# Expert slots of a whole layer in one list of 35 steps in place of two lists of 19

## The chip, the cores and the metric

The kernel runs on one core of a Trainium2 chip. The metric is the time of one execution on the device, in microseconds (us). A core has five engines with a queue of instructions each: TensorE (PE in the profile, its weight loads PEld), VectorE (DVE), ScalarE (ACT), GpSimd (POOL) and SyncE (SP), which here issues nearly all plain DMAs. Engines wait for each other by semaphores and each runs its own instructions in order.

## The reference

The input x has 2 x 2048 tokens of 256 values: 4096 tokens, 32 tiles of 128. Three layers follow one another, all in float32:

```
x = x + 0.5 * ffn(layernorm(x))
x = x + attention(layernorm(x))
x = x + 0.5 * ffn(layernorm(x))        (the same weights as the first)

ffn(h):  g   = softmax(layer_norm(h) @ router_w.T)      4 experts
         top two experts of each token, weights divided by their sum
         hid = relu(layer_norm(h @ w1[e]))              256 -> 512
         out = sum over the two of weight * (hid @ w2[e])  512 -> 256
         return layer_norm(out)
```

Attention is linear and causal, with 16 heads of 16. The change touches the two ffn layers.

## The kernel before

**Slots.** Each token is computed only for its two experts. A token and one of its experts make a slot, so a layer has 8192 slots. The rows of the tokens, split into a high and a low half-precision part, are scattered by indirect DMAs to `slots_in` in DRAM, where every expert has a region of its own. Two blocks of 128 slots of one expert are a slot tile (S2 = 256), and one step of the mixture computes one slot tile. Its results go to `slots_out`; later each token gathers its two rows and sums them with its weights.

**Two groups.** The 32 token tiles of a layer are two groups of 16 (GT). Each group has tables and buffers of its own. 16 token tiles fill 16 slot tiles, and since each expert's last one is only part filled, up to three more are needed: a group has NJ = 19 steps, whatever the router chooses, and a mixture has NP = 38. The list of a group (`tables`: expert and row of each step, read by SP and PE from `rtab` and `etab`) is made once all 16 tiles are routed. Four pads of zeros (`pads`) fill what is left of each expert's last slot tile.

**A step** p, by engine:
- SP stores the two halves of step p-1 (`store_slots`, L480), then loads step p+5 (`load_slots`): two transposed copies to hT (L466) and one plain copy to hs (L469). The first load of a group also writes the pads (L452) and waits for all scatters of the group (L461, L462). R_HT = 5 buffers hold hT, R_HS = 3 hs, R_Y = 4 the results.
- PE runs `grams` of p+2 (L1869, L1870) for the variance of the hidden row, `layer1` of p in two halves (L1893 to L1895), `std_T` of p+1 (L1881), and `layer2` of p-1 in two halves (L1908 to L1910), interleaved.
- DVE runs `variances` of p+2 (L915, L920), `relu_low` (L934), `std_parts` (L926, L927) and `twice_low` of p+3 (L906).
- ACT runs `relu_high` (L1451, two a step), `std_row` (L1444) and `scale_out` of p-1 (L1459).
- POOL raises the variances to a power, `pair_std` (L613).

**Beside the steps.** In the 19 steps of a layer's first group the second group is routed, one or two token tiles a step (`ROUTED`, steps 0 to 9): statistics for four tiles at a time (`quad_norm` L782 and L785, `quad_factors`), rows on ACT (L1420, L1427), their low part on DVE (L801), four transposes on PE with a copy by ACT (`row_T`, L1433), and logits. After an octet of tiles (steps 5 and 10) come `logits`, `choose`, `place`, then `scatter` of two tiles a step on POOL (two indirect DMAs a tile, L605), in steps 7 to 10 and 12 to 15. `tables` follows at step 12, `positions` and `gates` at step 13. In the steps of the second group the first group's outputs leave, one tile a step: `gather` (L629) on POOL, `first_weighted` (L1468) on ACT, `token_sum` and `token_out` on DVE (L950 to L965).

The first group of the first layer is routed in the preparation, together with the preparing of the weights (`weights`). The first group of the second layer is routed within attention, where the second group of the first layer leaves as well; its rows lie where W2 was, so that W2 is fetched again from DRAM afterwards (L501). The last group leaves in a tail after the last step (`gather_last`). In the first mixture `ahead` prepares attention: maxima and scales of its weights at steps 14 to 18, rows of its first tokens in the second group's steps (`rs` on POOL, L1606 on ACT, `rows_out_T` on PE, L1977).

Of SP's order before the change, the core is:

```
for p in range(p0, p1):
    if p > p0:
        store_slots(p - 1, 0)
        store_slots(p - 1, 1)
    if p + AHEAD < p1:
        load_slots(p + AHEAD)
```

## Time and profile before

| what | value |
|---|---|
| median of 3 runs | 1131.0 us (1130.91 to 1135.23) |
| profiled execution | 1138.73 us |
| its span | 1137.0 us |
| mean granted TensorE clock | 0.901 of full |
| busy: PE, DVE, ACT, POOL | 872.4, 732.4, 500.6, 561.3 us |
| bytes read from DRAM and written | 50.89 MB, 47.19 MB |

The span runs from the first to the last instruction of the program in the profiled execution; the time has what lies around it as well, and this execution was among the longer ones. "Busy" is time in which an engine has an instruction at work; waits of the sequencers and issuing of DMAs aren't counted. Matmuls overlap each other, so the mean duration of one, about 275 ns, is not its share of the time.

### The profile page before, as it was taken

The numbers are of one execution on the slowest core, as the hardware profiler recorded it, in microseconds if no ns is written. First come the engines' busy times: TensorE is split into PE (matmuls) and PEld (weight loads), VectorE is DVE, ScalarE is ACT, GpSimd is POOL, SyncE is SP. The second block draws the span as 40 slices with busy tenths as digits, with TensorE's granted clock in tenths as the row PEclk, the third lists the DMA queues.
The fourth block names the chain that finished last, engine by engine and source line by source line (L and its number), as shares of the span: only waits on it lengthen the run. The fifth ranks groups of instructions, "written<-read, shape, count | busy, mean of one in ns | idle before, by whom it ended". The sixth has DMA issues, their size and how long they took to land.

```text
span 1137.0 us, 26666 instructions
## 1 busy us (share of the span) xinstructions
PE 872.4 (77%) x8596; PEld 662.4 (58%) x8596; DVE 732.4 (64%) x2104; ACT 500.6 (44%) x958; POOL 561.3 (49%) x631
## 2 busy tenths in 40 slices
PE   1543499978999897798788787775799989999700
PEld 1432387856888774565555554443687778888500
DVE  4547776666777754598787764372675774878335
ACT  2642366422444454565565555430565333444311
POOL 4146224551456453687685366354226542555373
PEclk9956599999999998999899899995899999999955
DMA  8042654563566411111121112123645657666343
GB/s 296 10 158 111 157 155 127 152 168 106 130 158 163 130 63 24 40 40 46 43 51 46 23 44 68 31 77 107 159 103 158 155 154 155 163 159 151 118 131 107
DMA packets 191146, 126.06 MB, mean 111 GB/s; under 512 B 126373, under 2 KB 180905, under 8 KB 190633
## 3 DMA queue, kind: packets, MB, share of 16 engines
q1 hardware_dynamic: 177746, 89.72, 30.1%
q0 software_dynamic: 12288, 33.57, 10.1%
q8 instruction: 79, 1.29, 0.5%
q10 hardware_dynamic: 984, 1.07, 0.3%
q14 instruction: 49, 0.40, 0.1%
HBM read 50.89 MB, written 47.19 MB: 86 GB/s over the span
## 4 chain that ended last, share of the span: by engine, by line
PE 48%; DVE 14%; issue 13%; POOL 7%; ACT 6%; DMA 5%; SPq 3%; another core or an unknown queue 3%; ACTq 0%; DVEq 0%; POOLq 0%
PE banks L1908 4%; PE banks L1895 4%; PE banks L1893 4%; PE banks L1894 4%; PE banks L1910 4%; PE banks L1909 4%; PE banks L1993 4%; POOL slots_in L605 3%; PE banks L1995 3%; PE banks L2106 3%; PE banks L1994 3%; PE banks L1869 2%; PE banks L1870 2%; DMA area<-slots_out,pos 2%
## 5 line engine op out<-in xcount | busy, mean ns | idle before, releaser
L613 POOL TENSOR_TENSOR stds<-vare,expo 128x4 f32<-128x4 f32 x76 | 80.5, 1059 | 208.3 <-DVE vare L920 207.0
L1908 PE MATMUL banks<-w2all,area 128*128 x608 | 167.0, 275 | 6.3 <-DMA w2all<-w_kept 3.6
L1893 PE MATMUL banks<-area,w1h 128*128 128x256 f16 x608 | 169.1, 278 | 2.1 <-DVE area L934 1.9
L1895 PE MATMUL banks<-area,w1l 128*128 128x256 f16 x608 | 168.5, 277 | 0.9 <-issue 0.9
L1894 PE MATMUL banks<-area,w1h 128*128 128x256 f16 x608 | 168.9, 278 | 0.3 <-issue 0.2
L1910 PE MATMUL banks<-w2all,area 128*128 x608 | 166.7, 274 | 1.8 <-issue 1.8
L1909 PE MATMUL banks<-w2all,area 128*128 x608 | 166.7, 274 | 0.0
L934 DVE SCALAR_TENSOR_TENSOR area<-banks,area 128x512 f16<-128x512 f32 x152 | 104.4, 687 | 88.2 <-ACT area L1451 75.2
L1451 ACT ACTIVATE area<-banks 128x512 f16<-128x512 f32 x152 | 89.6, 590 | 123.8 <-PE banks L1895 99.8
L605 POOL DMA_INDIRECT slots_in<-area,spos x96 | 102.9, 1072 | 75.4 <-DVE spos L855 49.6
L737 POOL TENSOR_TENSOR area<-area 128x512 f16<-128x512 f32 x64 | 79.3, 1244 | 119.0 <-ACT area L1663 118.4
L1459 ACT ACTIVATE area<-banks,stds 128x256 f32<-128x256 f32 x152 | 70.9, 466 | 98.6 <-PE banks L1910 80.3
L629 POOL DMA_INDIRECT area<-slots_out,pos x96 | 97.0, 1010 | 25.8 <-issue 21.6
L1993 PE MATMUL banks<-area 64*128 64x32 f16 (+1 forms) x766 | 76.6, 226 | 41.5 <-issue 21.5
L1869 PE MATMUL banks<-gramh,area 128*128 x304 | 77.9, 290 | 24.9 <-issue 11.0
L1993 PEld LDWEIGHTS banks<-area 64*128 64x128 f16 (+1 forms) x766 | 39.9, 96 | 77.7 <-issue 51.0
L915 DVE CUSTOM_DVE_ANT_0 area<-banks,area 128x256 f16<-128x256 f32 x152 | 58.3, 420 | 33.0 <-PE banks L1870 27.2
L1995 PE MATMUL banks<-area 64*128 64x32 f16 (+1 forms) x766 | 75.9, 221 | 4.5 <-issue 4.5
L1870 PE MATMUL banks<-graml,area 128*128 x304 | 77.9, 291 | 0.6 <-issue 0.6
L1994 PE MATMUL banks<-area 64*128 64x32 f16 (+1 forms) x766 | 75.5, 222 | 2.2 <-issue 2.2
L1663 ACT ACTIVATE area<-area 128x512 f16<-128x512 f32 x64 | 40.1, 628 | 71.1 <-DVE area L1325 68.4
L1908 PEld LDWEIGHTS banks<-w2all,area 128*128 128x128 f16 x608 | 59.5, 98 | 19.5 <-issue 7.5
(278 smaller groups left out, 2226.3 us busy)
## 6 DMA issues: line engine op xcount, KB each, us to landing
area<-slots_in SPq DMA_DIRECT2D x76, 256.0 KB
slots_out<-area SPq DMA_DIRECT2D x152, 128.0 KB
X<-in_L_attn_x_dram SPq DMA_DIRECT2D x8, 512.0 KB, 6.1
slots_in<-zrow SPq DMA_DIRECT2D x16, 256.0 KB
area<-area SPq DMA_DIRECT2D x256, 16.0 KB
out_dram<-X SPq DMA_DIRECT2D x32, 128.0 KB
area<-slots_in SPq DMA_TRANSPOSE x152
area<-in_L_ffn_w_dram SPq DMA_DIRECT2D x4, 512.0 KB, 11.7
```

Of the source, the lines that this page charges most:

```text
L605: pool.indirect_dma_start(slots_in[G % 2], bass.IndirectOffsetOnAxis(spos[:, O % 2, k, j:j + 1], 0), rows_of(i).rearrange("p c d -> p (c d ...
L934: dve.scalar_tensor_tensor(out=Rl[:, p % 2, ms].rearrange("p m t -> p (m t)"), in0=bank[k][:, :], scalar=0.0, in1=Rh[:, p % 2, ms].rearran ...
L1869: pe.matmul(o, a[:, c], gramh[c][:, bass.ds(e, 1), :], start=(c == 0), stop=False)
L1893: pe.matmul(o, w1h[c][m][:, bass.ds(e, 1), :], a[:, c], start=(c == 0), stop=False)
L1894: pe.matmul(o, w1h[c][m][:, bass.ds(e, 1), :], a[:, KC + c], start=False, stop=False)
L1895: last = pe.matmul(o, w1l[c][m][:, bass.ds(e, 1), :], a[:, c], start=False, stop=(c == KC - 1))
L1908: pe.matmul(o, Rh[:, p % 2, k, rows], w2h[k][:, bass.ds(e, 1), :], start=(k == 0), stop=False)
L1909: pe.matmul(o, Rh[:, p % 2, k, rows], w2l[k][:, bass.ds(e, 1), :], start=False, stop=False)
L1910: last = pe.matmul(o, Rl[:, p % 2, k, rows], w2h[k][:, bass.ds(e, 1), :], start=False, stop=(k == HC - 1))
L1993: pe.matmul(o, lh, rh, start=start, stop=False, **kw)
L1994: pe.matmul(o, lh, rl, start=False, stop=False, **kw)
L1995: return pe.matmul(o, ll, rh, start=False, stop=stop, **kw)
```

## The change

A layer has one list of NP = NT + E - 1 = 35 steps for all its 32 token tiles, one `slots_in` and one `slots_out`. The list is made in three pieces, each as soon as its slots are certain:
- after the first octet, 8 token tiles: steps 0 to 4, slot tiles that this octet fills;
- after the second, 16 token tiles: steps 5 to 12, those filled by then;
- after all four: steps 13 to 34. It begins with the slot tiles that were part filled by the first 16 token tiles, so that by step 18 all slots of these are done, and the first half's outputs can leave from step 20.

The load of a step waits for the piece of the list and the scatters that it needs. The pads come once a layer, at SP's step 9, and slot tiles 13 and 14 are loaded at its step 10, each later one four steps ahead. Routing of the second half is done in steps 0 to 5, three token tiles a step (in order 3, 3, 2, 3, 3, 2), with the first rows ahead of step 0; octets are complete at steps 2 and 5, scatters take three tiles a step in steps 4 to 9, and the last tables are made at step 8. Two banks take turns for the transposed rows. On PE, `std_T` now stands ahead of `layer1`. The first half leaves in steps 20 to 32, two tiles in three of them. In attention the first octet gets its tables ahead of the second. The reload of W2 follows the first five loads as before, but waits for the scatters of attention by itself. `ahead` keeps its step numbers (the former second group's count on from 19, less three), and a spare region of zeros is written once at the start, for slot tiles past the last.

```diff
-    NJ = GT + E - 1
-    NP = 2 * NJ
-    REG = GT * P + S2
+    NO = NT // TO
+    NP = NT + E - 1
+    SPARE = NT * P + S2
+    REG = SPARE + (E - 1) * S2
+    PHASE = (0, TO - E + 1, GT - E + 1, NP)
+    SEGS = (1, 3, 4)
+    K1 = GT + E - 1
...
-        ROUTED = (0, 2, 3, 5, 6, 8, 10, 11, 13, 14, 16)
-        OCTET_AT = (5, 10)
-        C_AT = 1
+        ROUTED = (0, 3, 6, 8, 11, 14, 16)
+        OCTET_AT = (2, 5)
+        MOVED = (3, 3, 2)
+        LEFT = (2, 1, 1, 2, 1, 1, 2, 1, 1, 1, 1, 1, 1)
+        LAST_AT = 10
...
+        def started(j):
+            return ROUTED[max(0, min(j + 2, len(ROUTED) - 1))]
         def routed(j):
+            return range(started(j - 1), started(j))
+        def leaves(j):
+            k = j - K1 - 1
+            return range(sum(LEFT[:k]), sum(LEFT[:k + 1])) if 0 <= k < len(LEFT) else ()
...
             def load_slots(p):
+                f, j = p // NP, p % NP
+                if j in PHASE:
+                    sp.wait_ge(r_tab, 3 * f + PHASE.index(j) + 1)
+                if j == PHASE[0]:
+                    sp.wait_ge(sc_h[0], 32 * TO * (2 * f + 1))
+                if j == PHASE[1]:
+                    sp.wait_ge(sc_h[1], 32 * TO * (2 * f + 1))
+                if j == PHASE[2]:
                     for o in range(GO):
+                        sp.wait_ge(sc_h[o], 32 * TO * (2 * f + 2))
+                    sp.wait_ge(sc_p, 16 * E * (f + 1) + 16)
...
+            def load_at(j):
+                return j - AHEAD if j < PHASE[2] else max(j - AHEAD, LAST_AT, j - 4)
...
                 else:
+                    for o in range(GO):
+                        sp.wait_ge(sc_h[o], 32 * TO * 3)
                     sp.wait_ge(m_w2, 16)
                     sp.dma_start(w2flat, w2_kept).then_inc(m_w2, 16)
+                for j in range(NP):
+                    if j > 0:
+                        store_slots(p0 + j - 1)
+                    if j == LAST_AT - 1:
+                        pads(f)
+                    for i in range(NP):
+                        if load_at(i) == j:
+                            load_slots(p0 + i)
...
 (POOL, mixture)
+                for j in range(NP):
+                    if j < GQ:
+                        quad_again(Q1 + j)
+                    if j + 2 < NP:
+                        pair_std(p + 2)
+                    if j + 2 < GQ:
+                        quad_rstd(Q1 + j + 2)
+                    for t in moves(j):
+                        scatter(GT * (G + 1) + t)
+                    for t in leaves(j):
+                        gather(GT * G + t)
+                    for t in leaves(j - 1):
+                        token_rstd(GT * G + t)
...
 (DVE, mixture; the loop over j, in its order)
                 quad_norm(Q1)
+                quad_norm(Q1 + 1)
                 twice_low(p0)
...
+                    for t in leaves(j - 2):
+                        token_out(i0 + t)
+                    if j + 2 < NP:
+                        variances(p + 2)
+                    for t in tiles[:1]:
+                        row_low(i0 + GT + t)
                     relu_low(p, 0)
+                    if j == 0 and f == 0:
+                        positions(G)
+                    if j == 1 and f == 0:
+                        gates(G)
+                    if j == OCTET_AT[-1] + 3:
+                        tables(f, 2)
+                    if j == OCTET_AT[-1] + 4:
+                        positions(G + 1)
...
 (DVE, the preparation)
                 chain(0)
+                tables(0, 0)
...
                 chain(1)
-                tables(0)
+                tables(0, 1)
...
 (ACT, mixture)
+                    for t in leaves(j - 1):
+                        first_weighted(i0 + t)
+                    if j + 1 < NP:
+                        std_row(p + 1)
                     relu_high(p, 0)
...
 (PE, mixture)
+                    if j + 2 < NP:
                         e[p + 2] = expert(p + 2)
                         grams(p + 2, e[p + 2])
+                    if j + 1 < NP:
+                        std_T(p + 1, i1 + started(j - 2))
                     layer1(p, 0, e[p])
+                    for t in turn[:1]:
+                        pe.wait_ge(b_sdr, p + 2)
+                        row_T(i1 + t)
+                    if j > 0:
                         layer2(p - 1, 0, e[p - 1])
+                    for t in turn[1:2]:
+                        row_T(i1 + t)
+                    layer1(p, 1, e[p])
+                    for t in turn[2:]:
+                        row_T(i1 + t)
```

The new `tables` and `positions` work on the limits of these pieces (4, 12 or 16 numbers) and on all steps at once; `positions` has six operations on 192 or 256 elements, the last `tables` three on 352.

## Rows read from the trace of the kernel before

**Rows 1.** The page: the span, and TensorE's busy time.
```profile
span 1137.0 us, 26666 instructions
...
PE 872.4 (77%) x8596; PEld 662.4 (58%) x8596; DVE 732.4 (64%) x2104; ACT 500.6 (44%) x958; POOL 561.3 (49%) x631
```

**Rows 2.** Stages: length, busy PE, PEld, DVE, ACT, POOL, PE's clock, DMA share, GB/s.
```profile
0.00:134.00 134.00, 50.07 (x319) 38.85 (x320) 80.58 (x251) 49.63 (x89) 52.04 (x81) 0.76 0.43 141
...
829.00:901.00 72.00, 68.51 (x698) 57.15 (x697) 46.31 (x184) 39.01 (x80) 32.77 (x32) 1.00 0.55 138
946.00:1070.00 124.00, 122.60 (x1124) 104.56 (x1123) 87.26 (x270) 52.58 (x110) 59.55 (x65) 1.00 0.59 144
1070.00:1137.00 67.00, 1.85 (x17) 1.42 (x15) 27.60 (x84) 7.76 (x18) 35.26 (x36) 0.55 0.43 131
```

**Rows 3.** Timeline of PE: start, duration, instruction; first grams of two steps.
```profile
323.04 0.27 PE L1869 MATMUL banks<-gramh,area 128*128 x1
...
329.57 0.27 PE L1869 MATMUL banks<-gramh,area 128*128 x1
```

**Rows 4.** Groups of ACT, 829 to 901: count, busy, mean ns, idle before.
```profile
L1451 ACT ACTIVATE area<-banks 128x512 f16<-128x512 f32 x19 | 11.3, 595 | 21.0 <-PE banks L1895 13.8 <-remote 6.5 <-issue 0.7
...
L1433 ACT ACTIVATE area<-banks 128x512 f16<-128x512 f16 x11 | 6.5, 589 | 0.0
L1420 ACT ACTIVATE h<-X,xnr,xrs 128x256 f32<-128x256 f32 x10 | 5.9, 592 | 0.0
```

**Rows 5.** Windows, L1451 (relu_high) alone: length, busy (count), clock, DMA.
```profile
901.00:947.00 46.00, 7.16 (x12) 0.96 0.55 153
```

**Rows 6.** Waits from 797 to 829: total, times, longest.
```profile
PE banks L1908 <- DMA w2all<-w_kept: 3.6, 1, 3.6
```

**Rows 7.** Timeline of SP's queue at the second mixture's start.
```profile
782.00 2.60 SPq L466 DMA_TRANSPOSE area<-slots_in  x2
...
800.85 0.46 SPq L501 DMA_DIRECT2D w2all<-w_kept  x1
```

**Rows 8.** Chain that ended last, at the end of the preparation: start, length.
```profile
125.36 1.42 DVE xst L782 x4
126.80 0.39 DVE xmv L785 x4
```

**Rows 9.** Windows, the stretch of the first tables on DVE.
```profile
86.40:90.60 4.20, 0.00 (x0) 0.00 (x0) 3.68 (x23) 0.34 (x1) 2.87 (x3) 0.90 0.45 155
```

**Rows 10.** Groups of POOL, 853 to 930.
```profile
L605 POOL DMA_INDIRECT slots_in<-area,spos x32 | 34.4, 1074 | 13.7 <-issue 8.3 <-DVE spos L855 5.4
L613 POOL TENSOR_TENSOR stds<-vare,expo 128x4 f32<-128x4 f32 x10 | 10.7, 1073 | 16.5 <-DVE vare L920 16.4
```

**Rows 11.** Timeline of SP, two steps of the first mixture's second half.
```profile
319.31 2.53 SPq L466 DMA_TRANSPOSE area<-slots_in  x2
...
325.39 2.54 SPq L466 DMA_TRANSPOSE area<-slots_in  x2
```

**Rows 12.** Timeline of SP, pads and first load of the last list.
```profile
920.07 4.67 SPq L452 DMA_DIRECT2D slots_in<-zrow  x4
927.78 2.72 SPq L466 DMA_TRANSPOSE area<-slots_in  x2
```

**Rows 13.** Chain that ended last: landing of that load's second transpose.
```profile
929.31 2.68 DMA area<-slots_in
```

**Rows 14.** Windows around a stop of PE, columns as in rows 2.
```profile
249.00:254.00 5.00, 0.56 (x4) 0.09 (x2) 4.77 (x7) 0.47 (x1) 3.96 (x4) 0.96 0.82 241
254.00:257.00 3.00, 2.59 (x13) 1.86 (x14) 0.53 (x3) 0.00 (x0) 0.00 (x0) 0.50 0.73 251
```

**Rows 15.** Chain that ended last: gathers that it waited for.
```profile
364.07 4.56 DMA area<-slots_out,pos
...
959.14 5.59 DMA area<-slots_out,pos
```

**Rows 16.** Timeline of DVE: the twice_low that waited for that load.
```profile
933.80 0.69 DVE L906 SCALAR_TENSOR_TENSOR area<-area 128x512 f32<-128x512 f16 x1 [2.38 <-DMA area<-slots_in]
```

More of the change, by code:

```diff
@@ L1188, in mixture @@
                     relu_low(p, 1)
-                    if here and octet(j, 1) is not None:
+                    if octet(j, 1) is not None:
                         place(O1 + octet(j, 1))
+                    for t in tiles[2:]:
+                        row_low(i0 + GT + t)
+                    if octet(j, 0) is not None:
+                        logits(O1 + octet(j, 0))
                     if f == 0:
-                        ahead(g - G, j)
-                    if p + 3 < p0 + NP:
+                        ahead(j)
+                    if j + 3 < NP:
                         twice_low(p + 3)
@@ L1786, in router @@
                 if j == 0:
-                    wait(pe, r_cnt, O - 1)
+                    wait(pe, r_cnt, O - 1 if O < GO or beside(i) else O)
                 if i == 0:
```

444 lines of the change are left out of this document (210 added, 234 removed).

## The prediction

> **What bounds the kernel now.** First the page's header and TensorE's line [rows 1]: TensorE works 77% of a span of 1137.0 us. Such a mean hides the stages, so the table by stage is next [rows 2]: preparation to 134, the first mixture's 38 steps, attention, the second mixture to about 1070, and a tail of 67 us in which TensorE does next to nothing. In 946 to 1070 TensorE is busy 122.6 of 124 us at full clock: it bounds a step that has no routing in it. Its length is read from the first gram matmul of two steps [rows 3]: 329.57 - 323.04 = 6.53 us. From 829 to 901 there are 19 relu_high (two a step), so 9.5 steps in 72 us, 7.6 each [rows 2, 4]; ten tiles are routed there, so a tile costs (72 - 9.5 x 6.53) / 10 = 1.0 us with all its stalls. The steps in which the second half's list begins are longer: 901 to 947 has 12 relu_high, six steps, in 46 us, 6.8 above 6 x 6.53 [rows 5]. Preparation, attention and the tail are chains through several engines.
>
> **The change, part by part.** The sum is made against the profiled execution, 1138.7 us, which is 7.7 above the median of the runs shown (1131.0); the difference is then taken from the median.
>
> *Steps.* A mixture runs 35 instead of 38, in both layers: 6 x 6.53 = **-39.2** [rows 3]. The loads, stores, pair_std and ReLU work of these steps go with them, all beside TensorE.
>
> *W2 of the second layer.* TensorE waits 3.6 us for the reload [rows 6]. SP issues it at 800.85, behind the ten transposes that it began at 782.00, when the last scatter of attention had landed [rows 7]. The first five loads need only the first octet after the change, so SP has them out before that wait, and the reload follows it at once: **-3.6**. TensorE is not free of attention before 786, so nothing more is gained there.
>
> *The old boundary.* Its 6.8 us in the second mixture [rows 5] held pads, scatter wait and slow scatter steps; they are priced anew below, so **-6.8** (between 0 and -6.8). In the first mixture the same steps carry the attention scales, which stay at steps 14 to 17: 0.
>
> *Preparation.* quad_norm of a second quad now stands on VectorE before the first twice_low: statistics 1.42 and aggregation 0.39, 1.9 us with the guard, on the chain [rows 8]. There is a table more (for one octet), some 18 short VectorE instructions, as many as the old table, in whose stretch VectorE was busy 3.68 of 4.2 us [rows 9]. It stands where VectorE also waits for others, so I take half: 1.9. Together **+4** (1.9 to 7).
>
> *Routing three tiles a step.* In all the 16 tiles cost TensorE the same. ACT makes two row activations (L1420, and L1427 of the same size) and a copy (L1433) per tile, 0.59 each [rows 4]. Three tiles add 5.3 us to at most 52.58 / 19 = 2.8 us of a plain step [rows 2]: 8.1 us, just under TensorE's 6.53 plus its part of three tiles. In the first mixture VectorE also has positions in step 0, with six larger operations more. **+4** for both layers (0 to 12).
>
> *Scatters.* Three tiles are six indirect DMAs. 32 of them took 34.4 us with 8.3 us between them, 1.33 each; a pair_std takes 1.07 [rows 10]. That is 9.1 us of POOL a step, against 6.5 of TensorE in steps 7 and 8. pair_std stands first in POOL's step and is needed only in the next one, some 4 us later, which covers most of it: **+1** (0 to 10). Here a rule speaks against the change. In the rows the scatters run beside a VectorE that is busy 46.31 of 72 us, and their mean is 1.07 [rows 2, 10]: little blocking is seen. The Trainium skill, SBUF — State Buffer, section "SBUF: two separate sides", says that VectorE and GpSimd share one port pair under an exclusive lock, and that GpSimd can't write the descriptors of its DMAs while VectorE holds it. By the row the term is +1; by the rule it grows to that of rival D.
>
> *Tile 13.* The largest loss. SP writes the pads at step 9, behind the stores of tile 8, and loads tiles 13 and 14 only at step 10. SP gets to its load 2.35 us after the next TensorE step begins (325.39 against 323.04), or 2.8 (319.31, where the step began at 323.04 - 6.53 = 316.51) [rows 3, 11]. From the first pad to the load behind the pads it is 927.78 - 920.07 = 7.7 us [rows 12]. So the load of 13 begins 2.8 + 7.7 = 10.5 us after step 10 does, 4.0 into step 11; without pads it would be 2.8. It has landed at 929.31 + 2.68 = 931.99, 4.2 after its issue [rows 12, 13]. The grams of tile 13 are TensorE's first work of step 11, so it stops for 7.0 to 8.2 us, 7.5 taken. Behind them stand std_T, both layers, and so ACT, VectorE and the stores; nothing covers it. When TensorE had been busy 0.56 of 5 us (249 to 254), the granted clock stood at 0.50, the 1.2 GHz level, from 254 to 257 [rows 14]; 2.6 us of work at half speed lose 1.3. Two layers: 2 x 8.8 = **+17.5** (0, if work of other engines had stopped TensorE anyway, to 22).
>
> *Loads four ahead.* From tile 13 on, tile i is loaded at step i-4, not i-5. From the start of a TensorE step the load begins at 2.35 to 2.8 and lands 4.2 later, at 6.55 to 7.0; it is needed at 6.53 [rows 3, 11, 13]. A whole step of spare is gone; these two would be 0.0 and 0.5 late, 0.25 in the mean. Of 2 x 22 such steps, eight of the first mixture stand beside other stalls: 36 x 0.25 = **+9** (0 to 25).
>
> *Gathers.* 16 tiles leave in 13 steps, so some steps gather two. Two landings of a gather are on the chain now, 4.56 and 5.59 us [rows 15]. A second tile puts two more issues, 2 x 1.3 if they cost what a scatter does [rows 10], before the landing that ACT waits for: at step 21 of both mixtures and behind rs(0) of the first, at most 7.8, taken **+6** (0 to 14).
>
> *Attention.* Two tables for one on VectorE, the second longer: **+1** (0 to 4).
>
> Sum: -39.2 - 3.6 - 6.8 + 4 + 4 + 1 + 17.5 + 9 + 6 + 1 = -7.1. Profiled execution 1131.6; median 1131.0 - 7.1 = 1124.
>
> **The rivals.** (A) *Most of the gain stays.* If tile 13 and the loads four ahead cost nothing, since routing makes steps 7 to 10 slow enough for SP and POOL to keep up, the sum is -33.6: 1098. Against it: SP's order is fixed, and the store before the load needs layer 2 of the step before. Chance 0.16.
> (B) *Slower.* Place: the slot rows (hs), copied behind the two transposes. VectorE began twice_low at 933.80 on rows whose load began at 927.78, 6.0 us [rows 12, 16]. With four ahead they come 8.4 to 8.8 us after the start of a step, 1.9 to 2.3 into the step whose variances need them, and VectorE, in order, stands still before relu_low, token sums and std_parts. It decides when that outruns TensorE's slack. VectorE is busy 87.26 of 124 us in the second mixture's second half [rows 2], and its 16 tiles will fall on fewer steps. If each of the 44 steps loses 0.7, none hidden, it is 30.8 - 9 = 21.8 more: 1146; at 0.5, 1137. Chance 0.27.
> (C) *No difference to see.* The same terms, each stall somewhat larger (10 us at tile 13, 0.35 a step): 1131. Chance 0.19.
> (D) *The lock.* If a scatter is blocked about as long again as it takes, 32 x 1.0 us more a mixture, all on the way to tile 13, less what TensorE's spare covers, it is about +50: 1174. It is the mechanism of the skill page named above. Chance 0.04.
> That the change doesn't do what it says is no case: the counts of steps are constants in it.
>
> **How the numbers follow.** The forecast's own case (1109 to 1125) has 0.34. A measurement of this kernel can tell about 0.5%, 5.7 us, from no change. Faster: 0.34 + 0.16 = 0.50; same 0.19; slower 0.27 + 0.04 = 0.31. The range for 8 in 10 goes from 1098 (A) to 1146 (B at its full price).
>
> **What would show it.** 70 pair_std instead of 76; no wait for W2; at step 11 of each mixture grams that wait 7 to 8 us for slots_in, behind the zrow stores; steps of 6.5 to 7 from 13 on, with waits for slots_in; waits for gathers at steps 21 and 27. The forecast is wrong if the wait at step 11 is under 3 us, if the later steps take over 7.1, or if preparation grows by over 8.

## The result and the profile after

The kernel after takes 1169.6 us (median of 4 runs, 1166.0 to 1178.3); the kernel before, on the same chip, 1133.1 (4 runs). The ratio is 1.032, interval 1.025 to 1.040: slower by 36.5 us, where 7 us faster was forecast. The profiled execution took 1167.67, that of the kernel before 1138.73, so these two differ by 28.9 us where the medians differ by 36.5. Below, every ratio is taken against the kernel before on the same chip, and its difference from 1 times 1131 us is "its us".

The page of the kernel after, where the first two lines answer to [rows 1]:

```profile
span 1165.9 us, 25520 instructions
...
PE 852.1 (73%) x8236; PEld 636.6 (55%) x8236; DVE 734.1 (63%) x2108; ACT 491.8 (42%) x928; POOL 550.6 (47%) x625
```

TensorE stands still for 49 us more (span less busy time). Its busy time falls by 20 us only, though it runs 360 matmuls less, 60 a step, which at full clock are 39 us of work (122.60 us for 1124 matmuls in [rows 2]). By stage, from the first relu_high of a mixture to the first one of its last step (us):

```
            preparation  first mixture  attention  second mixture  tail   span
before         136.6         279.4        382.8        266.2       72.0  1137.0
after          138.7         299.5        382.7        272.4       72.6  1165.9
```

Of the 28.9 us of span, 26.3 are in the two mixtures, which have three steps less and are 20.1 and 6.2 us longer. The windows of the two mixtures, columns as in [rows 2], first of the kernel before, then of the kernel after:

```profile
136.60:416.00 279.40, 257.82 (x2385) 213.97 (x2383) 195.43 (x626) 128.24 (x262) 129.53 (x147) 0.97 0.54 139
798.80:1065.00 266.20, 251.70 (x2361) 210.75 (x2360) 182.38 (x597) 120.83 (x248) 120.47 (x122) 0.99 0.58 147
```

```profile
138.70:438.20 299.50, 251.59 (x2202) 203.41 (x2201) 190.69 (x607) 120.67 (x240) 123.22 (x143) 0.91 0.47 123
821.00:1093.00 272.00, 239.06 (x2172) 195.56 (x2170) 171.81 (x550) 112.81 (x225) 112.61 (x118) 0.96 0.48 129
```

The granted clock falls from 0.97 and 0.99 to 0.91 and 0.96. Since its levels are 1.0 and 0.5, the time at 0.5 (1.2 GHz) is twice what the mean lacks to 1, times the length: an estimate of 22 us before and 76 after. So a stop costs twice here, once as waiting and again when TensorE works on at 1.2 GHz behind it. About half of the 39 us that the removed steps saved went back in this way. But for tile 13 no term below shows it separately; in the experiments it is part of each time.

Step lengths, each from the first gram matmul of a step to that of the next, as in [rows 3], show where the steps grew:

```
first mixture, steps 0 to 10
before   9.1  7.1  7.7  7.1  7.7  7.9  7.5  7.9  7.5  8.7  6.8
after    9.5  9.7  7.3 10.0 14.0  9.2 10.1  6.6 10.0 14.8 13.5
steps 20 to 31
before   6.5  6.5  6.5  6.5  6.5  6.5  6.5  6.5  6.5  6.5 11.3  8.0
after    6.7  6.9 11.3  8.2  6.5  8.2  7.4 15.5  7.3  6.5  6.7  6.5

second mixture, steps 0 to 10
before   9.0 12.5  7.8  7.1  7.7  7.9  7.4  7.7  7.7  9.4  6.8
after    9.2  8.1  7.3 10.0  9.8  9.0 11.8  6.6  9.9 13.7 13.3
steps 20 to 31, where outputs leave
before   6.5  6.5  8.0  6.5  6.5  6.5  6.5  6.5  6.5  6.5  6.5  6.5
after    6.5  7.5  8.4  6.5  8.4 11.5  7.8  6.6  7.8  7.1  6.8  7.1
```

The plain steps between (13, 17 to 20 of the second mixture) are 6.5 to 6.6 again. Its step 1 has lost W2's wait of [rows 6] and is 4.4 us shorter.

**Tile 13.** The waits of the kernel after from 905 to 930 (total, times, longest), then SP's queue in the same stretch, which answers to [rows 12]:

```profile
PE banks L1942 <- DMA area<-slots_in: 6.4, 1, 6.4
```

```profile
914.38 3.59 SPq L471 DMA_DIRECT2D slots_in<-zrow  x4
918.01 1.51 SPq L503 DMA_DIRECT2D slots_out<-area  x2
920.75 2.55 SPq L489 DMA_TRANSPOSE area<-slots_in  x2
```

The grams of step 11 wait behind pads, stores and load, in that order: 6.4 us here and 6.8 in the first mixture, for 7 to 8.2 foreseen. Step 11, behind the wait, runs in part at 1.2 GHz and takes 8.8 and 8.6 us for a plain 6.5, with a granted clock of 0.72 in both; here the second:

```profile
924.80:933.40 8.60, 8.38 (x58) 6.43 (x59) 2.84 (x10) 2.26 (x4) 1.01 (x1) 0.72 0.39 105
```

**What was not foreseen** stands in front of it. GpSimd's queue in the kernel after, at its steps 7 and 8 of the second mixture: twelve scatters (L635) in two runs of six about one pair_std:

```profile
887.89 1.04 POOL L635 DMA_INDIRECT slots_in<-area,spos  x1 [0.20 <-issue]
...
894.30 0.96 POOL L635 DMA_INDIRECT slots_in<-area,spos  x1 [0.30 <-issue]
895.28 1.04 POOL L642 TENSOR_TENSOR stds<-vare,expo 128x4 f32<-128x4 f32 x1
896.52 1.04 POOL L635 DMA_INDIRECT slots_in<-area,spos  x1 [0.20 <-issue]
...
902.93 0.96 POOL L635 DMA_INDIRECT slots_in<-area,spos  x1 [0.30 <-issue]
```

TensorE in the same stretch, and ACT's relu_high:

```profile
893.20 0.27 PE L1968 MATMUL banks<-area,w1l 128*128 128x256 f16 x1
893.59 0.27 PE L1981 MATMUL banks<-w2all,area 128*128 x1
894.98 0.27 PE L1982 MATMUL banks<-w2all,area 128*128 x1 [1.12 <-issue]
895.09 0.27 PE L1983 MATMUL banks<-w2all,area 128*128 x1
895.71 0.27 PE L1981 MATMUL banks<-w2all,area 128*128 x1 [0.35 <-issue]
896.43 0.28 PE L1982 MATMUL banks<-w2all,area 128*128 x1 [0.45 <-issue]
...
903.18 0.58 PE L1954 MATMUL banks<-ident,s 128*1 128x128 f16 x4 [3.33 <-DVE s L988]
```

```profile
896.47 0.60 ACT L1522 ACTIVATE area<-banks 128x512 f16<-128x512 f32 x1 [5.19 <-remote]
...
905.19 0.60 ACT L1522 ACTIVATE area<-banks 128x512 f16<-128x512 f32 x1 [5.30 <-remote]
```

The window of that stretch, columns as in [rows 2]:

```profile
893.00:896.00 3.00, 1.39 (x9) 0.56 (x6) 0.00 (x0) 0.00 (x0) 2.64 (x3) 1.00 0.70 226
```

Until 893.2 a matmul follows the other every 0.11 us. Then, at full clock and with no wait named, matmuls start singly or in twos, 0.7 or 1.4 us apart, and relu_high comes 5.6 us after the matmul that it reads (L1968 at 890.58). This is called slow issue below. The second thing is the last line of TensorE's rows: std_T, which now stands ahead of layer1, waits 3.3 us for VectorE. VectorE's queue tells why:

```profile
897.10 0.69 DVE L995 SCALAR_TENSOR_TENSOR area<-banks,area 128x512 f16<-128x512 f32 x1 [6.73 <-issue]
897.71 0.15 DVE L888 TENSOR_TENSOR cnt<-carry,regbase 128x4 f32<-128x4 f32 x1
...
902.73 0.17 DVE L987 TENSOR_SCALAR s<-stds 128x2 f16<-128x2 f32 x1
902.93 0.20 DVE L988 SCALAR_TENSOR_TENSOR s<-stds,s 128x2 f16<-128x2 f32 x1
```

The last `tables`, 5.1 us, stands ahead of std_parts (L987, L988), which std_T needs. It begins so late because relu_low (L995) stands before it, which begins as the late relu_high ends.

The kernel before has the slow issue as well, where it scatters two tiles a step. TensorE and ACT in its first mixture, at the end of step 13 and in step 14:

```profile
238.52 0.27 PE L1870 MATMUL banks<-graml,area 128*128 x1 [0.38 <-issue]
239.25 0.27 PE L1869 MATMUL banks<-gramh,area 128*128 x1 [0.47 <-issue]
```

```profile
240.75 0.47 ACT L1459 ACTIVATE area<-banks,stds 128x256 f32<-128x256 f32 x1 [6.27 <-remote]
```

ACT stood idle for 6.27 us. So what the change adds is more of it, not something new.

**Gathers.** Waits of the kernel after from 1000 to 1093, then from 330 to 425. ACT waited for landings before as well (43.8 us in 16 times from 946 to 1066). New is that TensorE then waits for std_parts (L988), 6.9 us in each mixture, and in the first, at step 27, 6.1 us for the rows for attention (3.5 before).

```profile
ACT area L1539 <- DMA area<-slots_out,pos: 34.6, 13, 4.2
...
PE banks L1954 <- DVE s L988: 6.9, 5, 3.3
```

```profile
ACT area L1539 <- DMA area<-slots_out,pos: 31.9, 13, 6.5
...
PE banks L2048 <- ACT h L1680: 6.1, 1, 6.1
```

### The profile page after: what moved, and what is told of

The parts are those of the page before. It is cut to its first block, busy times and chain, and to the rows that moved or that the text cites. A ratio compares the mean times of both kernels' runs of the same rounds, so it can differ in the third digit from the quotient of the medians.

```text
span 1165.9 us, 25520 instructions
## 1 busy us (share of the span) xinstructions
PE 852.1 (73%) x8236; PEld 636.6 (55%) x8236; DVE 734.1 (63%) x2108; ACT 491.8 (42%) x928; POOL 550.6 (47%) x625
## 4 chain that ended last, share of the span: by engine, by line
issue 26%; PE 24%; DVE 17%; POOL 14%; DMA 7%; ACT 6%; SPq 4%; another core or an unknown queue 1%; DVEq 0%; ACTq 0%; POOLq 0%
POOL slots_in L635 5%; POOL stds L642 4%; DMA area<-slots_out,pos 4%; PE banks L2064 3%; PE banks L2177 3%; PE banks L2066 2%; PE banks L2065 2%; DMA area<-slots_in 2%; POOL area L659 2%; SPq L548 2%; PE banks L1824 1%; ACT area L1709 1%; SPq L489 1%; POOL area L718 1%
## 5 line engine op out<-in xcount | busy, mean ns | idle before, releaser
L642 POOL TENSOR_TENSOR stds<-vare,expo 128x4 f32<-128x4 f32 x70 | 73.2, 1045 | 272.0 <-DVE vare L981 272.0
L995 DVE SCALAR_TENSOR_TENSOR area<-banks,area 128x512 f16<-128x512 f32 x140 | 96.3, 688 | 112.0 <-ACT area L1522 82.6
L1967 PE MATMUL banks<-area,w1h 128*128 128x256 f16 x560 | 159.4, 285 | 1.9 <-issue 1.8
L1966 PE MATMUL banks<-area,w1h 128*128 128x256 f16 x560 | 160.1, 286 | 0.5 <-DVE area L995 0.5
L1968 PE MATMUL banks<-area,w1l 128*128 128x256 f16 x560 | 158.9, 284 | 1.4 <-issue 1.4
L1981 PE MATMUL banks<-w2all,area 128*128 x560 | 154.8, 276 | 3.3 <-issue 2.5
L1982 PE MATMUL banks<-w2all,area 128*128 x560 | 154.8, 276 | 2.0 <-issue 2.0
L1983 PE MATMUL banks<-w2all,area 128*128 x560 | 154.6, 276 | 0.6 <-issue 0.4
L635 POOL DMA_INDIRECT slots_in<-area,spos x96 | 97.7, 1017 | 67.2 <-DVE spos L879 39.4
L1522 ACT ACTIVATE area<-banks 128x512 f16<-128x512 f32 x140 | 82.6, 590 | 102.7 <-PE banks L1968 74.0
L1530 ACT ACTIVATE area<-banks,stds 128x256 f32<-128x256 f32 x140 | 65.6, 469 | 88.0 <-PE banks L1983 71.3
L1515 ACT ACTIVATE area<-banks 1x512 f16<-1x512 f16 x70 | 40.6, 580 | 97.6 <-PE banks L1954 79.6
L976 DVE CUSTOM_DVE_ANT_0 area<-banks,area 128x256 f16<-128x256 f32 x140 | 53.7, 421 | 26.9 <-PE banks L1943 14.4
## 6 DMA issues: line engine op xcount, KB each, us to landing
area<-in_L_ffn_w_dram SPq DMA_DIRECT2D x4, 512.0 KB, 11.4
area<-in_L_ffn_w_dram SPq DMA_DIRECT2D x2, 1024.0 KB, 14.8
```

The lines of the kernel that those rows point to most:

```text
L635: pool.indirect_dma_start(slots_in, bass.IndirectOffsetOnAxis(spos[:, O % 2, k, j:j + 1], 0), rows_of(i).rearrange("p c d -> p (c d)"), No ...
L642: pool.tensor_tensor(stds[:, p % R_SD], vare[:, p % 2].unsqueeze(2).to_broadcast([P, 2, 2]), expo[:, :].unsqueeze(1).to_broadcast([P, 2, 2 ...
L1966: pe.matmul(o, w1h[c][m][:, bass.ds(e, 1), :], a[:, c], start=(c == 0), stop=False)
L1967: pe.matmul(o, w1h[c][m][:, bass.ds(e, 1), :], a[:, KC + c], start=False, stop=False)
L1968: last = pe.matmul(o, w1l[c][m][:, bass.ds(e, 1), :], a[:, c], start=False, stop=(c == KC - 1))
L1981: pe.matmul(o, Rh[:, p % 2, k, rows], w2h[k][:, bass.ds(e, 1), :], start=(k == 0), stop=False)
```

## Experiments: the parts on the kernel before

Each of these puts one part of the change on the kernel before.

**Scatters of three tiles a step.**

```diff
 def moves(j):
-    if at + 2 <= j < at + 2 + TO // 2:
-        t = TO * o + 2 * (j - at - 2)
-        return t, t + 1
+    k = j - at - 2
+    if 0 <= k < 3:
+        return tuple(range(TO * o + 3 * k, TO * o + min(3 * k + 3, TO)))
```

> The kernel before, with its scatters three token tiles a step (3, 3, 2 in steps 7 to 9 and 12 to 14) and nothing else changed. Theory S (six indirect DMAs of POOL in a row, twelve and more in two steps, slow down the issue of instructions on TensorE, ScalarE and VectorE): each of the four octets loses some 3 to 5 us, the kernel is 10 to 20 us slower, with idle time marked issue or remote on PE and ACT while POOL scatters. Rival (the bursts are harmless; in the changed kernel tables and rows hold up the steps): within 3 us, or a few us faster, since the last scatter lands a step earlier.

Measured: 1157.39 us, ratio 1.0216 (1.0173 to 1.0258): +24.4. Steps 8 and 14 take 16.0 and 19.5 us in the first mixture, 15.5 and 18.5 in the second, for 7.5, 16.5, 7.7 and 11.1. GpSimd's own work, six scatters at 1.27 and a pair_std, is 8.7 us a step and can't make 16. TensorE of this kernel in step 14 of the second mixture, in the middle of its grams:

```profile
924.33 0.27 PE L1870 MATMUL banks<-graml,area 128*128 x1 [0.39 <-issue]
925.05 0.27 PE L1869 MATMUL banks<-gramh,area 128*128 x1 [0.45 <-issue]
926.47 0.27 PE L1870 MATMUL banks<-graml,area 128*128 x1 [1.15 <-issue]
927.21 0.27 PE L1869 MATMUL banks<-gramh,area 128*128 x1 [0.47 <-issue]
```

The same beat as in the kernel after. It lasts until 935.8, 1.4 us behind the end of the series of scatters. From 928 on the granted clock is 0.50, so the +24.4 hold slow work behind the gaps too.

**Three tiles routed a step**, octets and scatters where they were.

```diff
-ROUTED = (0, 2, 3, 5, 6, 8, 10, 11, 13, 14, 16)
+ROUTED = (0, 3, 6, 8, 8, 8, 11, 14, 16)
```

(and quad_norm, quad_factors and their powers in each step instead of every other one)

> The kernel before with three token tiles routed a step (3, 3, 2, none, none, 3, 3, 2) and the statistics of a quad in each step, the octets, tables and scatters where they were. My prediction priced the dense routing of the kernel after at +4 us for both layers; its first seven steps stood 24 us over the plain steps, with routing itself. Density theory: the six full steps take 10 us or more each, the free ones 6.5, and the sum is 5 to 15 us more, 1136 to 1146. Rival: ACT keeps up, 1131 to 1134.

Measured: 1148.3 us, ratio 1.0100 (1.0074 to 1.0126): +11.3. The steps that route three, three and two tiles take 10.7, 13.4, 8.0 and 10.0, 11.2, 8.9 in the second mixture; step 1 holds the wait for W2, and steps 0 and 1 took 9.0 and 12.5 without this. The time is within the 5 to 15 us expected, while the steps with two tiles stay under the 10 us. The cause shows in the waits: TensorE's transposes (L1777) wait 6.4 and 6.1 us for ACT's copy (L1433) in the two mixtures, for 1.3 and 1.0 in the kernel before.

**Outputs that leave in 13 steps.** `gather`, `first_weighted`, `token_sum` and `token_out` over the tiles of `leaves`, as in the kernel after:

```diff
+LEFT = (2, 1, 1, 2, 1, 1, 2, 1, 1, 1, 1, 1, 1)
...
-    t = j - C_AT
-    if 0 <= t < GT:
-        gather(GT * G + t)
+    for t in leaves(j):
+        gather(GT * G + t)
```

> The kernel before with the outputs leaving in 13 steps, two token tiles in three of them, as in the kernel after. If the density of the gathers made the gather steps of the kernel after slow (they took 21 and 14 us over 6.53 a step, 6 and 1 before), this one loses 10 to 28 us: 1141 to 1159. If the slower gather steps come from the other order of the engines' work or from the four-step loads, it stays at 1131 to 1134.

Measured: 1156.31 us, ratio 1.0166 (1.0133 to 1.0198): +18.8. TensorE's waits in its first mixture, 306 to 425:

```profile
PE banks L1896 <- DVE area L939: 6.0, 2, 4.9
PE banks L1980 <- ACT h L1609: 4.5, 1, 4.5
```

layer1 waits for relu_low (L939), which waits for relu_high, which stands behind the landing; and the rows for attention come late, as at step 27 of the kernel after. The steps one or two behind a pair of tiles take 9.3 and 14.2 us in the first mixture and 8.4, 11.0 and 8.7 in the second, and step 30 of the first 13.8 for 11.3.

**The weighting moved out of the way.** The last kernel, with ACT's `first_weighted` behind both relu_high and scale_out, and `token_sum` behind relu_low.

```diff
 (ACT)
-    for t in leaves(j - 1): first_weighted(i0 + t)
     relu_high(p, 0)
...
     scale_out(p - 1, 1)
+    for t in leaves(j - 1): first_weighted(i0 + t)
```

> The kernel before with the dense gathers (which cost 20 us), where ACT weights the gathered rows at the end of its step instead of ahead of relu_high, and VectorE sums them behind relu_low. If the loss comes from ACT waiting for the landing ahead of relu_high, so that TensorE stands still behind it, most of it goes: 1131 to 1141. If it comes from the gathers themselves (transfers, issue of GpSimd ahead of pair_std), it stays at 1150 to 1156.

Measured: 1152.47 us, ratio 1.0113 (1.0080 to 1.0147): +12.8 for +18.8. The two intervals overlap a little. In the first mixture step 28 falls from 14.2 to 9.3 us and step 30 from 13.8 to 10.4; in the second step 25 falls from 11.0 to 8.0 and step 21 rises from 8.4 to 10.4. So the landing ahead of relu_high is perhaps a third of the price. The rest stays with two tiles of gathers on GpSimd ahead of the next pair_std; which part of them isn't told apart.

**std_T and std_row first.** Before: `std_T` ahead of `layer1`, `std_row` ahead of `relu_high`.

```diff
+    std_T(p + 1, ...)
     layer1(p, 0, e[p])
-    std_T(p + 1, ...)
```

> The kernel before with std_T ahead of layer1 on PE and std_row ahead of relu_high on ACT, as the change has them. Theory T: slower by 8 to 20 us, in the steps of the second half, with waits of PE for the parts of the standard deviation after late gathers. Rival G: within 4 us of the kernel before, since one gather a step is early enough.

Measured: 1141.56 us, ratio 1.0083 (1.0051 to 1.0115): +9.4. That isn't all waiting at std_T: in the profile TensorE waits for std_parts (L927) 1.6 us in the first mixture and 2.3 in the second. The step that grew most, step 9 of the second mixture, 14.2 for 9.4, begins with gram matmuls 0.6 and 0.7 us apart with no wait named, and ACT's relu_high (L1451) starts late there twice, after 1.75 and 2.46 us idle marked remote. What the order costs apart from that isn't shown.

## Experiments: the parts undone in the kernel after

**std_T and std_row back behind.**

```diff
-    std_T(p + 1, i1 + started(j - 2))
     layer1(p, 0, e[p])
+    std_T(p + 1, i1 + started(j - 2))
...
-    std_row(p + 1)
     relu_high(p, 0)
+    std_row(p + 1)
```

> The changed kernel with std_T back behind the first half of layer1 on PE, and std_row back behind relu_high on ACT. Theory T (std_T ahead of layer1 takes from TensorE the 1.3 us in which std_parts used to arrive, so each late gather now stops it): the steps of the second half lose their waits of PE L1954 for DVE L988, 8 to 12 us less in each mixture, about 1150 in all against 1168. Rival G (the gathers two a step are what costs, wherever std_T stands): within 4 us of the changed kernel.

Measured: 1166.74 us, ratio 1.0344 (1.0272 to 1.0417): nothing gained, and the 8 to 12 us a mixture of theory T not there. In the kernel after the order by itself costs nothing that can be told.

**Pads and tile 13 one step earlier.**

```diff
-    if j == LAST_AT - 1:
+    if j == LAST_AT - 2:
         pads(f)
...
-    return j - AHEAD if j < PHASE[2] else max(j - AHEAD, LAST_AT, j - 4)
+    return j - AHEAD if j < PHASE[2] else max(j - AHEAD, LAST_AT - 1, j - 4)
```

> The changed kernel with the pads written at SP's step 8 and slot tile 13 loaded at its step 9. The wait of the grams of tile 13, 6.4 and 6.8 us in the changed kernel, is SP's order: it should shrink by 3 to 6 us in each mixture, 6 to 12 us in all, about 1158. If the wait is set by the scatters' landing instead, it stays above 5 us and the time within 3 us of the changed kernel.

Measured: 1159.21 us, ratio 1.0236 (1.0192 to 1.0280): +26.7, so 9.8 of the 36.5 go. Step 10 falls from 13.5 and 13.3 to 8.5 and 7.7, and step 11 to 6.5 in both. Step 9 of the first mixture grows from 14.8 to 17.1. The intervals of the two kernels overlap a little; the step lengths don't leave the gain in doubt.

**With that, outputs thinned,** the last tile weighted, summed and put out behind the last step:

```diff
-LEFT = (2, 1, 1, 2, 1, 1, 2, 1, 1, 1, 1, 1, 1)
+LEFT = (2,) + 14 * (1,)
```

> The kernel after with the pads and tile 13 one step earlier (1159 by itself) and the first half leaving one tile a step up to the last step, the last tile behind it. If the 20 us that dense gathers cost in the kernel before are the same 20 us here, it comes to about 1140, less what the last tile adds behind the last step (2 to 5 us): 1140 to 1146. If the gather steps of the kernel after are long for another reason, it stays at 1155 or above.

Measured: 1159.99 us beside 1138.73 of the kernel before, ratio 1.0143 (1.0080 to 1.0206): +16.2, 10.5 less than without. That is about half of what dense gathers cost on the kernel before, with intervals that overlap a little; 1140 to 1146 us was expected, so the dense gathers cost less here than there.

**With the pads at step 8, the last octet two tiles a step** in steps 7 to 10, tile 13 at step 10 as in the kernel after:

```diff
-MOVED = (3, 3, 2)
+MOVED = ((3, 3, 2), (2, 2, 2, 2))
```

> The kernel after with the pads at step 8 and tile 13's load left at step 10, and the last octet scattered two tiles a step in steps 7 to 10 instead of three in steps 7 to 9. If six scatters a step make the 14 us steps, those at 9 and 10 fall to under 9 us in both mixtures, and against the kernel with only the pads earlier (1.024 of before) it gains 8 to 14 us less what tile 13 waits for its later scatters (2 to 8 us): 1.012 to 1.022. If they stay at 14 us, the spacing isn't the cause in the kernel after: 1.024 or above.

Measured: 1166.25 us, ratio 1.0302 (1.0237 to 1.0366), +34.2: no gain that can be told against the kernel after, and 7.5 us more than with the pads and tile 13 a step earlier. By what was set down before, this speaks against the spacing of the scatters as the cause in the kernel after. Its steps say more. Step 8 falls to 6.8 and 6.6, for 10.0 and 9.9, and TensorE has no gap without a named wait there, though relu_high still comes 2.8 us behind its matmul (888.80, L1968 at 885.73). But step 9 stays at 13.2 and 13.9 and step 10 takes 15.9 and 15.1. Its waits from 886 to 924:

```profile
PE banks L1942 <- DMA area<-slots_in: 8.4, 1, 8.4
...
PE banks L1954 <- DVE s L988: 4.5, 1, 4.5
```

The first has grown from 6.4, since tile 13's load waits for the last two tiles' scatters, which come a step later. The second is `tables` ahead of std_parts. So on the way to tile 13 the kernel after has three stops behind one another, and thinning one of them uncovers the others. That reading fits the steps; what the six scatters a step cost in the kernel after by themselves is not shown.

## Experiments: what the slow issue needs

All put work beside the kernel before, in the second mixture alone; the scatters write to tensors that nobody reads.

**Six scatters more in each of steps 16 and 17**, in which nothing is routed:

```diff
+if f == 1 and g == G and j in (16, 17):
+    for t in range(3):
+        for k in range(2):
+            pool.indirect_dma_start(more[6 * (j - 16) + 2 * t + k], ..., rows_of(3 * GT + TO + t), None)
```

> The kernel before with twelve more scatters of the usual size (128 rows of 1 KB, to tensors that nobody reads), six in each of steps 16 and 17 of the second mixture, where nothing is routed. Theory S (scatters issued one behind the other by GpSimd slow the issue of all engines): each of these two steps or the one behind grows as in the kernel before with three tiles a step, together 10 to 25 us over the 13 us that two plain steps take; 1141 to 1156. Rival P (GpSimd is merely busy, and pair_std late behind 7.6 us of scatters): 7.6 + 1.1 = 8.7 us a step for 6.5, together 4 to 5 us; 1135. Rival 0: nothing, 1131.

**Six powers of 128x4 on GpSimd instead:**

```diff
+    for t in range(6):
+        pool.tensor_tensor(busy_out[:, 6 * (j - 16) + t], capn[:, 0:4], nhalf[:, :], ALU.pow)
```

> The same steps with six powers of 128x4 numbers a step on GpSimd in place of the six scatters, about 1.06 us each, so 6.4 us of GpSimd and no DMA. Theory S expects no slow issue here: at most 7.5 us a step, 1131 to 1134. Rival P, for which the time of GpSimd is the cause, expects the same loss as with the scatters.

**Scatters of rows of 64 bytes instead** (the source is `rows_of(3 * GT + TO + t)[:, 0, 0:D // 8]`):

> The same twelve scatters with rows of 64 bytes in place of 1 KB: as many descriptors, a sixteenth of the bytes. If the issuing or the descriptors slow the engines (S1), the loss is that of the full scatters, 10 to 25 us. If it is the bytes that fill the DMA engines (S2), the steps stay under 9 us each and the time is 1131 to 1136.

**Twelve plain copies by SP instead,** behind its loads of these steps:

```diff
+    for t in range(6):
+        sp.dma_start(more[6 * (p - p0 - 16) + t], zrow[:, :]).then_inc(s_more, 16)
```

> Twelve plain copies of 128 rows of 1 KB from SBUF to DRAM issued by SP in the same two steps: the bytes of the twelve scatters, none of GpSimd's issuing. S1 expects no slow issue, though SP's own loads may come late: up to 5 us, 1131 to 1136. S2 expects 10 to 25 us as with the scatters.

Measured: 1.0029 (0.9999 to 1.0060), 1.0002 (0.9973 to 1.0031), 1.0021 (0.9979 to 1.0063) and 1.0041 (1.0007 to 1.0075). I expected slow issue from the first; it gave 3 us, near rival P's size, with an interval that holds 0, and none of the four shows single steps over 10.5 there. Step 16 takes 10.2 in the first, but also 10.3 and 10.5 in other kernels of this document that add nothing at that step. Small rows and large ones can't be told apart at this size. By these four my theory would have fallen. Its series holds the same numbers, with one difference:

```profile
921.05 1.04 POOL L669 DMA_INDIRECT more<-area,spos  x1 [0.20 <-issue]
922.39 1.96 POOL L669 DMA_INDIRECT more<-area,spos  x1 [0.30 <-issue]
924.66 0.96 POOL L669 DMA_INDIRECT more<-area,spos  x1 [0.30 <-issue]
```

In each of its two runs of six one scatter took 1.96 us; in the series beside which TensorE went slow all took 0.96 to 1.04. Which is cause and which effect isn't shown, and series with neither stand in the traces too (eight scatters from 883 to 894 in the kernel with the last octet two tiles a step). The window from 930 of the kernel with the twelve large scatters, columns as in [rows 2], shows that a full DMA alone doesn't do it; in the slow stretch of the kernel after the DMA share was 0.70:

```profile
930.00:935.00 5.00, 4.67 (x43) 3.85 (x41) 3.21 (x5) 1.80 (x4) 4.19 (x4) 1.00 0.86 246
```

**Two scatters more beside the four in steps 7 to 9 and 12 to 14**, and the same with two powers in their place:

```diff
+if f == 1 and g == G and j in (7, 8, 9, 12, 13, 14):
+    for k in range(2):
+        pool.indirect_dma_start(more[2 * n + k], ...)
```

> The kernel before with two more scatters of full size (to tensors that nobody reads) in each of steps 7, 8, 9, 12, 13 and 14 of the second mixture alone, behind the four that are there: six a step for GpSimd, as in the kernel before with three tiles a step, but in the steps that route. Theory B (six indirect DMAs a step beside routing slow the issue of all engines, wherever they write): steps 8 and 14 of the second mixture take 14 us or more for 7.5 and 11, the time grows by 10 to 20 us, 1141 to 1151. Rival C (twelve more in plain steps cost 2 to 5 us, so it isn't the number, but something of the real scatters): up to 5 us, 1131 to 1136.

> The same steps with two powers on GpSimd, 1.06 us each, in place of the two scatters. Theory B expects no slow issue and less than 4 us, 1131 to 1135. If it is the lateness of pair_std behind a full GpSimd, the loss is nearly that of the scatters.

Measured: 1161.61 us, ratio 1.0188 (1.0136 to 1.0241), +21.3; and 1140.78 us, 1.0021 (0.9985 to 1.0056). Twelve DMAs that nobody waits for until the end cost about 21 us (15 to 27 by the interval), in steps 8, 10 and 14 (16.7, 11.4 and 16.8 for 7.7, 6.8 and 11.1). Two powers there, about the same time of GpSimd without DMAs, cost nothing that can be told. TensorE of the first of these kernels in step 8:

```profile
868.50 0.27 PE L1918 MATMUL banks<-w2all,area 128*128 x1 [1.17 <-issue]
869.22 0.27 PE L1919 MATMUL banks<-w2all,area 128*128 x1 [0.46 <-issue]
869.93 0.28 PE L1920 MATMUL banks<-w2all,area 128*128 x1 [0.44 <-issue]
```

**Six more in each of steps 3 and 4**, where tiles are routed and nothing else is scattered, and **in steps 24 and 25**, beside gathers. The edit is that of steps 16 and 17 with these conditions (and rows of zeros as the source in the first):

```diff
+if f == 1 and g == G and j in (3, 4):
...
+if f == 1 and g == G + 1 and j in (5, 6):
```

> The kernel before with six more scatters of 1 KB rows (zeros, to tensors that nobody reads) in each of steps 3 and 4 of the second mixture, where three tiles are routed and GpSimd issues no other scatter. If it is routing beside six scatters that slows the issue, two steps there grow by 8 us or more together, as at steps 8 and 14. If it is the length of an unbroken series (steps 12 to 15 and their neighbours hold 16 or more), each grows by under 2.5 us, as in steps 16 and 17.

> Six more scatters in each of steps 24 and 25 of the second mixture, where a tile leaves a step (two gathers and a power more for GpSimd): eight indirect DMAs a step, about 12.4 us of GpSimd for a step of 6.53, and nothing routed. By GpSimd's time alone the two steps and the one behind grow by about 12 us together. If the slow issue needs only the number of indirect DMAs, by 20 us or more, with single steps of 14 us and TensorE's matmuls some 0.7 us apart.

Measured: 1.0062 (1.0037 to 1.0087), +7.0, with steps 4 and 5 at 13.1 and 10.0 for 7.7 and 7.9 and matmuls 0.7 and 1.4 us apart from 826.1 to 829.7. And 1.0100 (1.0043 to 1.0157), +11.3, with steps 25 to 27 at 11.4, 13.4 and 7.9, 13.1 over plain ones. The two steps of the first grow by 7.5 us together, just under the 8 that stood for this theory, and far over the 2.5 each of the other. It says that a series of six beside routing is enough. The second, with two executions only, gives what GpSimd's time alone would; the beat shows in it as well (3.6 us of gaps, 984.6 to 989.8), but the time doesn't need it.

What the runs show: beside six indirect DMAs of GpSimd a step, issued one behind the other, TensorE's issue can be slow for 4 to 12 us; it takes neither the real destination nor readers, and powers in their place don't do it. Open stays why steps 16 and 17 escaped, and by what path it comes about. Plain copies of the same bytes were put only in steps 16 and 17, where the scatters were harmless too, so whether it is GpSimd's issuing or the transfers beside those of a routing step isn't separated.

## Experiment: a version faster than both

The kernel before with two transfers moved: W2's reload behind three of the five first loads, and the second list's pads at SP's step 12.

```diff
 for p in range(p0, p0 + AHEAD):
     load_slots(p)
+    if f == 1 and p == p0 + 2:
+        sp.wait_ge(m_w2, 16)
+        sp.dma_start(w2flat, w2_kept).then_inc(m_w2, 16)
...
-    else:
-        sp.wait_ge(m_w2, 16)
-        sp.dma_start(w2flat, w2_kept).then_inc(m_w2, 16)
...
+    if p == p0 + OCTET_AT[-1] + 2:
+        pads(2 * f + 1)
```

> The kernel before with its two late transfers moved: the pads of the second list at SP's step 12 instead of ahead of its first load at step 14, and the reload of W2 behind three of the five first loads. By the rows of before, 3.6 us of waiting for W2 go, and the first load of the second list comes up to 4.7 us earlier where it is on the path (surely the second mixture, perhaps not the first, where the attention scales are made at the same steps): 1123 to 1128. Rival: that load waits for the last scatter of step 15 and not for the pads, and only the W2 wait goes: 1128. Rival: the reload delays two loads of the first steps by as much: 1131.

Measured: 1127.67 us against 1136.18 of the kernel before on the same chip, ratio 0.9925 (0.9899 to 0.9952): 8.5 us faster. SP's queue at the start of its second mixture:

```profile
793.19 0.46 SPq L490 DMA_DIRECT2D w2all<-w_kept  x1
```

The reload is issued 7.7 us earlier than in [rows 7], and step 1 of the second mixture takes 7.1 for 12.5 us. That is 5.4 of the 8.5; the rest isn't placed, and the interval reaches from 5.4 to 11.4. The pads moved and gained nothing: steps 14 to 17 take 32.7 us for 32.1, for the load waits for the last scatter.

## Why the prediction was wrong

By its own steps:
- *Steps*, -39.2: right; the plain steps are 6.53 us and three fewer a layer. This is TensorE's work at full clock.
- *W2*, -3.6: right and too small. Step 1 is 4.4 us shorter in the kernel after, 5.4 in the version above.
- *The old boundary*, -6.8: not tested by itself. Its steps are gone, but the steps that took its work over are longer than it was.
- *Preparation*, +4: 2.1. *Attention*, +1: 382.7 for 382.8.
- *Routing three a step*, +4 (0 to 12): 11.3 on the kernel before, at the end of its range. I summed ACT's time against TensorE's and took the difference; that TensorE's transposes wait for ACT's copy was not in that sum, and they wait 12.5 us there for 2.3.
- *Scatters*, +1 (0 to 10): 24.4 on the kernel before. **This step failed most.** The working was right about GpSimd, 8.7 to 9.1 us a step. That the other engines go slow beside it was in no term of mine, though the kernel before shows it (ACT idle for 6.27 us at 240.75). In the kernel after the 24.4 aren't shown: there four scatters a step instead of six in one octet gave nothing that can be told.
- *Tile 13*, +17.5 (0 to 22): the waits are 6.8 and 6.4 us where 7.5 was taken. Step 11 behind them is 2.3 and 2.1 over the plain 6.5 at a clock of 0.72, where 1.3 was taken. That makes 17.6, and earlier pads give 9.8 of it back. The mechanism was right.
- *Loads four ahead*, +9: TensorE waits for slots_in in all 9.1 us (3 times) in the first mixture and 11.1 (8 times) in the second, so 7.0 beside tile 13's 13.2. About right. The sign that the later steps take over 7.1 came all the same: steps 13 to 31 of the second mixture are 7.3 us in the mean, by the steps where outputs leave.
- *Gathers*, +6 (0 to 14): 18.8 on the kernel before, 10.5 given back by thinning in the kernel after. I priced the landing alone; layer1 behind relu_low behind relu_high stood 4.9 us in one place.
- Missing altogether: the clock behind every stop but tile 13's. By the estimate above, 22 us of the mixtures ran at 1.2 GHz before and 76 after, tile 13's among them. And std_T ahead of layer1 with the last `tables` ahead of std_parts: the order alone goes with +9.4 on the kernel before and nothing in the kernel after; with tables before it TensorE waits 3.3 us in the second mixture.

With the waits and the prices on the kernel before, the sum is -39.2 - 3.6 - 6.8 + 2.1 + 11.3 + 24.4 + 13.2 + 7.0 + 18.8 + 9.4 = +36.6, against 36.5 measured. So close a fit is luck, and it doesn't prove the list complete. Each term has 3 to 7 us of its own; 4.4 us of clock behind tile 13 are left out; the 9.4 of the order didn't come back when it was undone in the kernel after, and thinning the gathers gave back 10.5, not 18.8. What the kernel after itself shows is 9.8 us of pads and tile 13 and about 10.5 of gathers. Dense routing and the first octet's scatters were never undone in it. The error lies in the steps that became denser (routing, scatters, gathers: +11 forecast, +54 on the kernel before), each read as busy time of one engine.

Rival A's sum, 1131.0 - 33.6, is 1097.4, where 1098 was written; nothing hangs on it. Of the rivals, B's mechanism (slot rows four ahead) is not it: steps 17 to 20 of the second mixture, which load four ahead, are 6.5 to 6.6. D named the right place and the right sign, and nearly the right time, with the wrong mechanism. The rule of the Trainium skill, SBUF — State Buffer, section "SBUF: two separate sides", is that GpSimd can't write descriptors while VectorE holds the port pair that they share. Here no lengthening is seen: the mean of the 32 scatters after, from 853 to 915, is 978 ns for the 1074 of [rows 10]:

```profile
L635 POOL DMA_INDIRECT slots_in<-area,spos x32 | 31.3, 978 | 9.5 <-issue 9.5
```

GpSimd wasn't held up; TensorE and ACT were, and VectorE behind them.

## What to carry to other kernels

A schedule that packs the same work into fewer steps is to be priced by the queue that every step goes through, not by the busy time of the engine that gets more: on the kernel before three packings cost 11, 24 and 19 us, more than the 39 us of the removed steps. Put each packing on the old kernel by itself first; a change of a few lines shows its price, if not yet what it will cost beside the others. Read the granted clock of the stages with the waits: here half of the saved work went back to a slower clock. And look at what SP has queued ahead of a transfer that somebody waits for: moving one reload gained more than the change.

## What the runs showed of the hardware

- Twelve scatters more, two beside the four of six steps, +21.3 us; twelve powers of GpSimd there, +2.4 with an interval that holds 0. In these stretches TensorE's matmuls start 0.7 or 1.4 us apart instead of 0.11, at full clock at first; in the kernel before with three tiles a step the clock is 0.92 from 924 to 928, with TensorE busy 1.35 of 4 us, and 0.50 from 928 to 936.
- Four scatters a step go with it too, for a shorter time: 0.7 us apart from 238.5 to 240 in the kernel before.
- DMA share 0.86 and 246 GB/s beside TensorE busy 4.67 of 5 us: full DMA engines alone don't slow its issue.
- The same number of DMAs in steps 16 and 17 cost 3 us, with an interval that holds 0. Their number in a step alone doesn't decide.
- Nearly every scatter takes 0.96 to 1.04 us; 1.96 is rare, two of the twelve in steps 16 and 17 and none in the mixtures of the kernel after. They start 1.27 us apart when nothing else is queued.
- Tile 13's wait of 6.4 us is followed by a step at a granted clock of 0.72.
